# A rebuilt opening of a graph attention kernel: rows of h prepared two parts ahead, and the second quad of h turned by the DMA queue

## The chip, the cores and the metric

The kernel runs on one core of one Trainium2 chip. The metric is the device time of one execution in microseconds (us). The times and the trace are those of the kernel before the change.

## The reference, cut to what matters

```python
h = relu(layernorm(x))                     # x: 4096 x 512, f32
q = h @ W_q.T + b_q;  k = h @ W_k.T + b_k;  v = h @ W_v.T + b_v
z = (q @ k.T) / sqrt(512)                  # 4096 x 4096
s = z * adj                                # adj: 4096 x 4096 of 0 and 1, f32, sparse
s = where(s == 0, -10000, s)
out = x + relu(softmax(s, axis=1) @ v)
```

The kernel never forms q and k. With M = W_k.T W_q the scores are h M h.T plus a term of the keys, (h . w), in which w comes from b_q and W_k; another vector u comes from b_k and W_q. M is a product of two f32 matrices (16 matmuls of 128x128 by 128x512). The other large products take f16 pairs (a high and a low half, three matmuls in the place of one).

## The kernel before, in words

**Tiles.** The 4096 rows are 32 tiles of 128, in 8 quads of 4 tiles, and in 16 pairs of 2. A block is 512 query rows. For the block's 512 columns, each pair of key tiles gives scores by seven products instead of eight (the functions `scores` and `product`, a Strassen-like scheme of 42 matmuls with 256 columns). After the opening, a main loop of 128 steps does for each step the scores of one pair (19 pairs ahead) and four products with v (`weigh_v`).

**Opening.** It makes M, w and u, normalises x into h, turns h so that its 512 features lie on the partitions, and makes for each tile `v` (`project_v`, 12 matmuls, 2.6 us) and for each quad and chunk of 128 features `g = M h` (`project_g`, 12 matmuls, 2.6 us). It is written out as "parts" k = 0, 1, 2, ...; part k = 4 g + i has the tile k for v, the chunk i of the quad g - 1 for g, and from part 9 on half of a pair's scores. Each engine has its own list of what it does in part k, in an order written by hand; nothing else schedules.

**One tile's way.** VectorE takes the statistics of a quad of x (`row_stats`, `aggregate`, `quad_var`), ScalarE the root (`square_root`), VectorE refines it (`quad_rstd`). ScalarE writes the normalised rows (`normalise`), then their high half (`high_h`), VectorE their low half (`low_h`) and the product with w (`row_dot`). Tiles 0 to 7 are turned by TensorE as f32 into PSUM (`transpose_h`) ahead of the split. The tiles from 8 on are split as rows into one of four row buffers and turned by a transposing DMA of SyncE's queue (`turn_h`). In part k the engines prepare tile k + 4.

**g.** ScalarE copies a chunk out of PSUM (`copy_g`), VectorE forms the four sums (`combine_g`, after chunks 1 and 3), ScalarE the high and VectorE the low half (`high_g`, `low_g`). In part 4 g this is done for the second half of the quad g - 2, and the scores of part 4 g + 1 wait for it. `store_g` writes the two pairs to DRAM.

**SyncE** issues every DMA from one list in order. An instruction that waits holds all that stand behind it. x is double buffered by quads; `load_x(q)` waits until the last tile of quad q - 2 is normalised.

**Scale.** Both v's weights and M are scaled by a power of two before the split. For that VectorE finds the largest absolute value, and GpSimd the largest over the partitions. w and u come from TensorE: four f32 matmuls each with 512 columns.

Of the kernel before, what the change touches and what calls it, by code (L numbers as in the profile page):

```python
# [5 lines left out]
F32 = mybir.dt.float32  # L6
# [5 lines left out]
ABSMAX = bass.bass_isa.ReduceOp.absmax  # L12
# [17 lines left out]
TURNED = 2 * QUAD  # L30
ROW_BUFS = 4
# [14 lines left out]
TINY = 1e-30  # L46
EXPONENT = 0x7F800000
WARM_UPS = 9
HEADROOM = (16.0, 4.0)
# [5 lines left out]
def adj_preln_attention(nc, x, adj_t, wq, bq, wk, bk, wv_t, bv, out, g_dram, v_dram, h_dram):  # L55
# [15 lines left out]
    with ctx:  # L71
# [16 lines left out]
        o_rows = sb("o_rows", [P, QUAD, DIM], F32)  # L88
        run_min = sb("run_min", [P, 2, QW], F32)
# [9 lines left out]
        zeros = sb("zeros", [P, P], F32)  # L99
        log_p = sb("log_p", [P, 1], F32)  # L100
# [7 lines left out]
        mag = [sb("mag_v", [P, KC], F32), sb("mag_m", [P, KC + 1], F32)]  # L108
        mag_all = [sb("mag_all_v", [P, KC], F32), sb("mag_all_m", [P, KC + 1], F32)]
# [24 lines left out]
        wv_pair = in_slots(16, 2).bitcast(F16).rearrange("p (s k n) -> p s k n", s=2, k=KC)  # L134
        m_pair = in_slots(18, 2).bitcast(F16).rearrange("p (s k n) -> p s k n", s=2, k=KC)
# [11 lines left out]
        h_rows = in_slots(10, 2).bitcast(F16).rearrange("p (u s n) -> p u s n", u=ROW_BUFS, s=2)  # L147
        p_hi = [p_buf[:, u, :, :] for u in range(3)]
        p_lo = [p_buf[:, 3 + u, :, :] for u in range(2)]
        x_quad = [o_rows[:, :, :],  # L150
# [4 lines left out]
        u_row = run_min[0:1, 0, :]  # L155
        bq_wide = row_acc[:, :].rearrange("p (k n) -> p k n", k=KC)
# [8 lines left out]
        u_row_bank = d_bank[0:1, :]  # L165
# [26 lines left out]
        wide_ready = sem("wide_ready")  # L192
# [5 lines left out]
        u_row_ready = sem("u_row_ready")  # L198
        u_row_copied = sem("u_row_copied")
# [4 lines left out]
        mag_ready = sem("mag_ready")  # L204
        mag_reduced = sem("mag_reduced")
# [136 lines left out]
        def gT_bank(q, i):  # L342
            return o_bank[1] if i % 2 == 1 else o_bank[3]
# [19 lines left out]
        def _(sp):  # L363
# [56 lines left out]
            def turn_h(t):  # L420
# [6 lines left out]
                sp.dma_start(quad_h(q)[:, :, :, span], h_rows[:, t % ROW_BUFS, :, :].rearrange("p s n -> p (s n)"),  # L427
# [10 lines left out]
            def store_out(s, a):  # L438
# [16 lines left out]
            load_first_x(1)
            load_wk(2)
            load_wk(3)
            load_first_x(2)
            load_first_x(3)
            for e in range(KC):  # L460
                sp.dma_start(wq_raw[:, e, :], wq[e * P:(e + 1) * P, :]).then_inc(wq_loaded[e], 16)
            sp.dma_start(wv_raw, wv_t.rearrange("(k p) n -> p k n", p=P)).then_inc(wv_loaded, 16)
            load_x(1)
# [5 lines left out]
            for g in range(QUADS + 1):  # L469
                if 1 <= g < QUADS:  # L470
                    store_h(g)
# [4 lines left out]
                if g >= 2:  # L476
                    store_g(2 * (g - 2))
                    store_g(2 * (g - 2) + 1)
                if 2 <= 2 * g - 3 < PAIRS:
                    load_adj(2 * g - 3)  # L480
                if 1 <= g < QUADS - 1:
                    turn_h(QUAD * g + QUAD)
                    turn_h(QUAD * g + QUAD + 1)
                if g < QUADS:
                    store_v(2 * g)
                if 1 <= g < QUADS - 1:
                    turn_h(QUAD * g + QUAD + 2)
                if g + 3 < QUADS:
                    load_x(g + 3)
                if 1 <= g < QUADS - 1:  # L490
                    turn_h(QUAD * g + QUAD + 3)
                if 2 <= 2 * g - 2 < PAIRS:
                    load_adj(2 * g - 2)
            store_g(PAIRS - 2)
# [39 lines left out]
        def _(pool):  # L534
            nc.gpsimd.memset(zeros[:, :], 0.0).then_inc(zeros_ready, 1)
            nc.gpsimd.memset(ident[:, :], 0.0).then_inc(ident_zero, 1)
# [19 lines left out]
            for k in range(2):  # L556
                pool.wait_ge(mag_ready, k + 1)
                nc.gpsimd.partition_all_reduce(mag_all[k][:, :], mag[k][:, :], P, ABSMAX).then_inc(mag_reduced, 1)
# [7 lines left out]
        def _(pe):  # L566
            def transpose_h(t):
                pe.wait_ge(normed, t + 1)
                if t >= 2:
                    pe.wait_ge(h_lo_ready, t - 1)  # L570
                if 2 <= t < QUAD + 2:
# [5 lines left out]
            def project_v(t):  # L577
# [4 lines left out]
                pe.wait_ge(wv_lo_ready, KC)  # L582
# [12 lines left out]
                for k in range(KC):  # L595
                    for m, (a, b) in enumerate(HI_LO):
# [4 lines left out]
            def project_g(q, i):  # L601
# [8 lines left out]
                elif q == 0 and i == 1:  # L610
                    pe.wait_ge(h_lo_ready, TURNED)
                else:
# [82 lines left out]
            def product_m(d):  # L695
                for e in range(KC):
                    if d == 0:
                        pe.wait_ge(wq_loaded[e], 16)
                    mm = pe.matmul(m_bank[d][:, :], wk_raw[:, e, d * P:(d + 1) * P], wq_raw[:, e, :],  # L699
                                   start=(e == 0), stop=(e == KC - 1))  # L700
                mm.then_inc(m_ready, 1)
# [4 lines left out]
            pe.wait_ge(wide_ready, KC)  # L706
# [948 lines left out]
```

## Time and profile before

| | |
|---|---|
| median of 3 runs | 1463.7 us (1463.51 to 1463.74) |
| profiled execution, its own time | 1463.89 us |
| its span in the trace | 1462.1 us |
| TensorE busy | 1449.8 us (99%) |
| VectorE busy | 1301.7 us (89%) |
| ScalarE busy | 868.2 us (59%) |
| granted TensorE clock | nine tenths or more of full speed in all 40 slices |

Busy time is the union of an engine's instructions. What a row calls idle is the time just before an instruction on the same engine. The first 300 us hold the opening; the main loop takes the rest.

### The profile page before, as it was taken

To read this page: it belongs to the slowest core of one execution; us is meant where nothing else is said; L and a number is where in the kernel's file an instruction comes from. 1 tells how busy PE (TensorE), PEld (TensorE's weight loads), DVE (VectorE), ACT (ScalarE), POOL (GpSimd) and SP (SyncE) were. 2 spreads that over 40 slices of the span, in tenths; PEclk is the share of its full clock that TensorE was granted. 3 is DMA by queue.
4 is the path that set the end of the run, shared out by engine and by line. 5 is a ranking of instruction groups with operands and counts; after the bars stand their busy time and mean duration, and the time that the engine had idled before them with its cause. 6 is when DMAs were issued, how large, how long until landed. Compare 5 with 4: busy or idle time off the path is not lost.

```text
span 1462.1 us, 24721 instructions
## 1 busy us (share of the span) xinstructions
PE 1449.8 (99%) x9414; PEld 924.2 (63%) x9414; DVE 1301.7 (89%) x1597; ACT 868.2 (59%) x1398; POOL 44.8 (3%) x27
## 2 busy tenths in 40 slices
PE   8999999999999999999999999999999999999999
PEld 4455556766666666666666666666666666666555
DVE  7979888898999899998989898989898999987986
ACT  4666666765656566655665565656566566655542
POOL 0000000000000000100010001000000001000100
PEclk9999999999999999999999999999999999999999
DMA  6587666375555665566556664666456655664252
GB/s 209 162 270 215 219 182 244 137 297 187 223 216 226 215 241 216 220 218 243 204 202 248 224 233 186 225 245 239 188 225 245 234 187 203 245 216 178 90 162 97
DMA packets 100533, 307.53 MB, mean 210 GB/s; under 512 B 33856, under 2 KB 34112, under 8 KB 98624
## 3 DMA queue, kind: packets, MB, share of 16 engines
q1 hardware_dynamic: 100416, 305.96, 58.5%
q8 instruction: 75, 1.23, 0.3%
q14 instruction: 42, 0.34, 0.1%
HBM read 260.84 MB, written 38.80 MB: 205 GB/s over the span
## 4 chain that ended last, share of the span: by engine, by line
PE 93%; DVE 4%; ACT 1%; issue 1%; DMA 0%; SPq 0%; POOL 0%; DVEq 0%; ACTq 0%
PE o L688 45%; PE za L630 22%; PE zd L630 11%; PE zb L630 5%; PE o L617 4%; PE o L597 4%; PE zb L688 1%; DVE stats L1117 1%; PE za L699 0%; DVE g_buf L1197 0%; DMA slots<-in_L_gnn_W_q 0%; ACT g_buf L839 0%; DVE slots L1291 0%; DVE slots L1169 0%; DVE slots L1287 0%
## 5 line engine op out<-in xcount | busy, mean ns | idle before, releaser
L688 PE MATMUL o<-v_buf,p_buf 128*128 128x512 f16 x3072 | 726.4, 376 | 0.8 <-DVE p_buf L1323 0.6
L688 PEld LDWEIGHTS o<-v_buf,p_buf 128*128 128x128 f16 x3072 | 300.5, 98 | 260.9 <-issue 1.5
L630 PE MATMUL za<-h_buf,g_buf 128*128 128x256 f16 x2952 | 402.2, 273 | 1.6 <-ACT um_tmp L888 0.7
L630 PEld LDWEIGHTS za<-h_buf,g_buf 128*128 128x128 f16 x2952 | 287.3, 98 | 140.0 <-DVE g_buf L1197 3.7
L630 PE MATMUL zd<-h_buf,g_buf 128*128 128x256 f16 x1476 | 201.3, 273 | 0.0
L908 ACT ACTIVATE slots<-slots,log_p 128x1024 f32<-128x1024 f32 x128 | 146.0, 1141 | 51.5 <-DVE slots L1316 51.4
L1323 DVE TENSOR_TENSOR p_buf<-slots,p_buf 128x1024 f16<-128x1024 f32 x128 | 157.4, 1230 | 14.5 <-PE zb L688 13.6
L1316 DVE TENSOR_TENSOR slots<-slots,floor_b 128x1024 f32<-128x1024 f32 x128 | 170.0, 1330 | 0.3 <-POOL floor_b L547 0.3
L1279 DVE TENSOR_TENSOR slots<-um_tmp,dm_tmp 128x512 f32<-128x512 f32 x128 | 89.2, 697 | 78.7 <-ACT dm_tmp L893 78.7
L903 ACT ACTIVATE slots<-za,c_all,kappa 128x256 f32<-128x256 f32 x128 | 72.2, 564 | 142.4 <-PE za L630 141.5
L1291 DVE SCALAR_TENSOR_TENSOR slots<-slots 128x1024 f32<-128x1024 f32 x128 | 156.0, 1219 | 0.2
L630 PEld LDWEIGHTS zd<-h_buf,g_buf 128*128 128x128 f16 x1476 | 144.4, 98 | 16.7
L866 ACT ACTIVATE mm_tmp<-za,c_all,kappa 128x256 f32<-128x256 f32 x128 | 72.5, 567 | 137.3 <-PE za L630 134.1
L915 ACT CAST p_buf<-slots 128x1024 f16<-128x1024 f32 x128 | 133.0, 1039 | 9.1 <-PE zb L688 8.6
L1337 DVE TENSOR_TENSOR acc<-acc,slots 128x1024 f32<-128x1024 f32 x112 | 137.1, 1224 | 0.3
L1303 DVE TENSOR_TENSOR run_min<-run_min,slots 128x1024 f32<-128x1024 f32 x112 | 136.4, 1218 | 0.2
L1287 DVE TENSOR_TENSOR slots<-slots,adj_own 128x1024 f32<-128x1024 f32 x92 | 115.8, 1259 | 12.7 <-ACT slots L903 5.1
L878 ACT ACTIVATE um_tmp<-za,c_all,kappa 128x256 f32<-128x256 f32 x128 | 72.5, 566 | 55.4 <-PE za L630 50.8
L888 ACT ACTIVATE um_tmp<-za,c_all,kappa 128x256 f32<-128x256 f32 x128 | 72.4, 566 | 54.1 <-PE za L630 53.7
L630 PE MATMUL zb<-h_buf,g_buf 128*128 128x256 f16 x738 | 100.7, 273 | 0.0
L630 PEld LDWEIGHTS zb<-h_buf,g_buf 128*128 128x128 f16 x738 | 72.2, 98 | 8.3
L597 PE MATMUL o<-slots,h_buf 128*128 128x512 f16 x288 | 66.1, 379 | 1.3 <-DVE v_buf L1177 1.3
(155 smaller groups left out, 1121.8 us busy)
## 6 DMA issues: line engine op xcount, KB each, us to landing
g_buf<-g_dram SPq DMA_DIRECT2D x108, 896.0 KB, 5.5
v_buf<-v_dram SPq DMA_DIRECT2D x128, 512.0 KB, 3.4
adj_own<-in_adj SPq DMA_DIRECT2D x92, 512.0 KB, 6.2
spare<-in_adj SPq DMA_DIRECT2D x36, 512.0 KB, 6.3
g_dram<-g_buf SPq DMA_DIRECT2D x12, 896.0 KB, 5.5
v_dram<-v_buf SPq DMA_DIRECT2D x16, 512.0 KB, 4.7
spare<-in_x SPq DMA_DIRECT2D x15, 512.0 KB, 7.5
h_buf<-h_dram SPq DMA_DIRECT2D x7, 1024.0 KB, 8.8
```

Source lines behind the costliest of these rows:

```text
L597: mm = pe.matmul(v_bank(t)[:, :], h[:, a, k, span], wv_pair[:, b, k, :], start=(k == 0 and m == 0), stop=(k == KC - 1 and m == 2))
L630: mm = pe.matmul(bank[:, 0:QH], g_of(i)[:, a, op, j, :], right[b][j], start=(fresh and j == 0 and m == 0), stop=(j == 1 and m == 2), skip_ ...
L688: mm = pe.matmul(bank, a[:, kt, span], v_buf[:, n % V_BUFS, kt, b, c:d], start=(j == 0 and kt == 0 and m == 0), stop=(j == PAIRS - 1 and k ...
L908: nc.scalar.activation(slot(n), slot(n), ACT.Exp, bias=log_p[:, 0:1], scale=-UNIT).then_inc(p_ready, 1)
L915: nc.scalar.copy(p_hi[n % 3], slot(n)).then_inc(p_hi_ready, 1)
L1279: v.tensor_tensor(slot(i)[:, 1, :], um_tmp[:, :, :].rearrange("p a n -> p (a n)"), dm_tmp[:, :, :].rearrange("p a n -> p (a n)"), ALU.add) ...
L1287: v.tensor_tensor(slot(i), slot(i), adj_buf[adj_slot(i)], ALU.mult).then_inc(weighted, 1)
L1291: v.scalar_tensor_tensor(out=slot(i), in0=slot(i), scalar=0.0, in1=slot(i), op0=ALU.is_equal, op1=ALU.subtract).then_inc(negated, 1)
L1303: v.tensor_tensor(run_min[:, :, :], run_min[:, :, :], slot(i), ALU.min).then_inc(min_seen, 1)
L1316: v.tensor_tensor(slot(n), slot(n), floor_b[:, :].unsqueeze(1).to_broadcast([P, 2, QW]), ALU.add).then_inc(lowered, 1)
L1323: v.tensor_tensor(p_lo[n % 2], slot(n), p_hi[n % 3], ALU.subtract).then_inc(p_lo_ready, 1)
L1337: v.tensor_tensor(acc[:, :, :], acc[:, :, :], slot(n), ALU.add).then_inc(summed, 1)
```

## The change

Five edits to the opening. The main loop is not touched.

1. **Loads.** `b_q` and `b_k` come laid out as 128 x 4, and the halves of W_k and W_q come in turns. W_v comes ahead of the last quarter of W_k and W_q.
2. **M, w and u.** The 16 f32 products run quarter by quarter as the weights land. w and u are summed by ScalarE and VectorE over the four quarters (`add_w`, `add_u`), and TensorE sums over the partitions with a matrix of ones: one matmul for w and four with one column for u.
3. **Scale.** The largest absolute value gives way to a root of the sum of squares: five ScalarE instructions with squares, one matmul with one column, one all-reduce of GpSimd.
4. **h of the second quad** goes the way of the later ones: `TURNED` is 4 now, so TensorE transposes tiles 0 to 3 only, and tiles 4 to 31 are turned by the DMA queue, from two row buffers.
5. **Two parts ahead.** In part k the engines prepare tile k + 2. The statistics of a quad move from the parts with i = 1 to those with i = 3, `quad_rstd` from i = 3 to i = 1, `key_terms` from i = 3 to i = 1, the root from i = 2 to i = 0.

```diff
-TURNED = 2 * QUAD
-ROW_BUFS = 4
+TURNED = QUAD
+ROW_BUFS = 2
...
+        def row_tile(k):
+
+            return k + 2 if k + 2 < TILES else -1
...
+            products_m(0, 0, 3)
+            products_m(1, 0, 3)
+            products_m(2, 0, 3)
+            pe.wait_ge(ones_ready, 1)
+            pe.wait_ge(square_v_ready, 1)
+            pe.matmul(norm_bank, ones[:, :], square[0][:, 0:1], start=True, stop=True).then_inc(square_v_summed, 1)
+            pe.wait_ge(w_part_ready, KC)
+            pe.matmul(w_bank[:, :], ones[:, :], w_part, start=True, stop=True).then_inc(w_ready, 1)
+            products_m(3, 0, 0)
             pe.wait_ge(ident_ready, 1)
             transpose_h(0)
+            products_m(3, 1, 2)
             transpose_h(1)
...
+            products_m(3, 3, 3)
+            pe.wait_ge(u_part_ready, KC)
             for d in range(KC):
-                mm = pe.transpose(u_bank[:, d:d + 1], u_row[:, d * P:(d + 1) * P], ident[0:1, 0:1])
+                mm = pe.matmul(u_bank[:, d:d + 1], u_part[:, d * P:(d + 1) * P], ones[:, 0:1], start=True, stop=True)
             mm.then_inc(u_ready, 1)
...
+            for t in range(QUAD):
+                project_v(t)
+                if t + 2 < TURNED:
+                    transpose_h(t + 2)
...
             def magnitude(k):
-                dve.wait_ge(mag_reduced, k + 1)
-                link(v.tensor_reduce(top[k][:, :], mag_all[k][:, :], AX_X, ALU.max))
+
+                dve.wait_ge(norm_ready, k + 1)
...
-                if i == 3 and 1 <= g and g + 2 < QUADS:
-                    quad_rstd(g + 2)
...
+                if i == 1 and g + 1 < QUADS:
+                    quad_rstd(g + 1)
...
-                if g + 1 < QUADS:
-                    low_h(k + QUAD)
+                if row_tile(k) >= 0:
+                    low_h(row_tile(k))
...
-                if g >= 2 and i == 1 and g + 2 < QUADS:
+                if i == 3 and g + 2 < QUADS:
                     for t in range(QUAD):
                         row_stats(QUAD * (g + 2) + t)
```

**VectorE, parts 15 and 16** (L1287/L1333 weighs a pair by adj, L1153/L1202 is `row_dot`, L1291/L1337 negates, L1182 to L1190 or L1231 to L1239 `combine_g`). Before:

```order
L1287 TENSOR_TENSOR slots<-slots,adj_own 128x1024
L1153 SCALAR_TENSOR_TENSOR half_min,dots<-acc,floor_b 128x512
L1291 SCALAR_TENSOR_TENSOR slots<-slots 128x1024
L1160 TENSOR_SCALAR c_all<-dots,bq_bk 128x4
L1182 TENSOR_TENSOR slots<-slots 128x256
```

and now:

```order
L1333 TENSOR_TENSOR slots<-slots,adj_own 128x1024
L1202 SCALAR_TENSOR_TENSOR half_min,dots<-acc,floor_b 128x512
L1337 SCALAR_TENSOR_TENSOR slots<-slots 128x1024
L1166 BN_STATS stats<-p_buf 128x6 x4
L1172 BN_AGGR mean_var<-stats 128x2 x4
L1177 COPY mean<-mean_var 128x4
L1178 TENSOR_SCALAR var_eps<-mean_var 128x4
L1231 TENSOR_TENSOR slots<-slots 128x256
```

The ten instructions of the statistics now stand between the negation of part 15 and the sums of g in part 16. Before they stood two parts earlier.

**SyncE, from the load of the third quad of x on.** Before:

```order
L370 DMA o_rows<-in_x 128x4x512
L380 DMA adj_own<-in_adj 128x1024 x2
L414 DMA v_dram<-v_buf 128x2048
L370 DMA p_buf<-in_x 128x4x512
L436 DMA h_dram<-h_buf 128x4096
L414 DMA v_dram<-v_buf 128x2048
L427 DMA_TRANSPOSE h_buf<-slots 128x8x128 x2
```

and now:

```order
L384 DMA o_rows<-in_x 128x4x512
L394 DMA adj_own<-in_adj 128x1024 x2
L428 DMA v_dram<-v_buf 128x2048
L441 DMA_TRANSPOSE h_buf<-p_buf 128x8x128
L441 DMA_TRANSPOSE h_buf<-h_row_own 128x8x128
```

The first transposes, those of tiles 4 and 5, stand right behind the load of x, two loads of adj and a store of v.

**SyncE, group g = 3** (L418/L432 is `store_g`). Before:

```order
L418 DMA g_dram<-g_buf 128x3584
L418 DMA g_dram<-spare 128x3584
L380 DMA adj_own<-in_adj 128x1024
L427 DMA_TRANSPOSE h_buf<-slots 128x8x128 x2
L414 DMA v_dram<-v_buf 128x2048
```

and now:

```order
L432 DMA g_dram<-g_buf 128x3584
L432 DMA g_dram<-spare 128x3584
L441 DMA_TRANSPOSE slots<-p_buf 128x8x128
L384 DMA p_buf<-in_x 128x4x512
L394 DMA adj_own<-in_adj 128x1024
L441 DMA_TRANSPOSE slots<-h_row_own 128x8x128
```

The transpose behind the stores was that of tile 16, used in part 16. Now it is that of tile 14, used in part 14.

## Rows read from the trace of the kernel before

**Rows 1.** The page: the chain that ended last, by engine.
```profile
PE 93%; DVE 4%; ACT 1%; issue 1%; DMA 0%; SPq 0%; POOL 0%; DVEq 0%; ACTq 0%
```

**Rows 2.** Stretches: length, each engine's busy time, clock, DMA share, GB/s.
```profile
31.50:47.00 15.50, 14.84 (x77) 7.63 (x75) 14.57 (x38) 8.73 (x16) 0.39 (x1) 1.00 0.26 101
47.00:60.70 13.70, 13.27 (x61) 5.77 (x62) 13.27 (x37) 7.83 (x13) 0.00 (x0) 1.00 0.66 194
60.70:73.00 12.30, 10.68 (x48) 4.52 (x48) 11.47 (x26) 8.98 (x16) 0.00 (x0) 1.00 0.55 129
104.00:134.50 30.50, 30.35 (x184) 17.52 (x182) 26.10 (x55) 20.50 (x36) 0.00 (x0) 1.00 0.74 232
```

**Rows 3.** The timeline of TensorE, opening: start, duration, instruction.
```profile
16.19 3.59 PE L717 MATMUL zd<-slots,b_cols 128*1 128x512 f32 x8
19.71 1.09 PE L574 MATMUL o<-ident,acc 128*128 128x128 f32 x8
24.51 3.70 PE L699 MATMUL zb<-slots 128*128 128x512 f32 x8
31.48 2.75 PE L597 MATMUL o<-slots,h_buf 128*128 128x512 f16 x12
73.11 0.83 PE L630 MATMUL za<-h_buf,g_buf 128*128 128x256 f16 x6 [0.68 <-DVE g_buf L1197]
```

**Rows 4.** DMA of the first 20 us: GB/s in 0.5 us, one issue.
```profile
GB/s 0 0 0 1 28 127 373 209 315 254 207 42 87 242 348 402 393 393 406 397 406 410 410 402 381 389 389 385 381 389 385 389 393 385 393 381 356 148 25 33
slots<-in_L_gnn_W_v SPq DMA_DIRECT2D x1, 1024.0 KB, 8.4
```

**Rows 5.** The scales of v's weights (timeline), and a wide ScalarE group (page).
```profile
23.77 2.56 ACT L926 ACTIVATE slots<-slots,up 128x512 f16<-128x512 f32 x4
26.58 2.73 DVE L1390 SCALAR_TENSOR_TENSOR slots<-slots,up 128x512 f16<-128x512 f32 x4
...
L908 ACT ACTIVATE slots<-slots,log_p 128x1024 f32<-128x1024 f32 x128 | 146.0, 1141 | 51.5 <-DVE slots L1316 51.4
```

**Rows 6.** The timeline of parts 13 to 17: VectorE, ScalarE, TensorE.
```profile
113.12 2.47 DVE L1117 BATCH_NORM_STATS2 stats<-p_buf 128x6 f32<-128x512 f32 x4
116.05 0.42 DVE L1182 TENSOR_TENSOR slots<-slots 128x256 f32<-128x256 f32 x1
129.16 0.42 DVE L1182 TENSOR_TENSOR slots<-slots 128x256 f32<-128x256 f32 x1
131.47 1.76 ACT L839 CAST g_buf<-slots 128x896 f16<-128x896 f32 x2
133.57 0.83 PE L630 MATMUL za<-h_buf,g_buf 128*128 128x256 f16 x6
```

**Rows 7.** TensorE: the scores of part 13, and v of tile 14.
```profile
103.19 0.83 PE L630 MATMUL za<-h_buf,g_buf 128*128 128x256 f16 x6
112.31 2.75 PE L597 MATMUL o<-slots 128*128 128x512 f16 x12
```

**Rows 8.** Stores of g (page); one store, the transpose behind it, one alone.
```profile
g_dram<-g_buf SPq DMA_DIRECT2D x12, 896.0 KB, 5.5
...
L418 SPq DMA_DIRECT2D g_dram<-g_buf x1: 1240/1240/1240, 74.4 to 74.4; - x1
DMA to landing us min/median/max: 7.7/7.7/7.7
...
L427 SPq DMA_TRANSPOSE slots<-slots x1: 2765/2765/2765, 75.7 to 75.7; - x1
DMA to landing us min/median/max: 9.1/9.1/9.1
...
L427 SPq DMA_TRANSPOSE h_buf<-slots x1: 1244/1244/1244, 151.7 to 151.7; - x1
DMA to landing us min/median/max: 3.1/3.1/3.1
```

**Rows 9.** VectorE's idle time in part 28.
```profile
229.16 0.69 DVE L1177 TENSOR_TENSOR v_buf<-o,v_buf 128x512 f16<-128x512 f32 x1 [1.71 <-ACT v_buf L816]
```

More of the change, by code:

```diff
@@ L99, in adj_preln_attention @@
         zeros = sb("zeros", [P, P], F32)
+        ones = sb("ones", [P, P], F32)
         log_p = sb("log_p", [P, 1], F32)
@@ L693, in weigh_v, with products_m @@
                 mm.then_inc(o_done, 1)
[L695 to L698, printed above, removed]
+            def products_m(e, first, last):
+                pe.wait_ge(wk_loaded[e], 16)
+                pe.wait_ge(wq_loaded[e], 16)
+                for d in range(first, last + 1):
                     mm = pe.matmul(m_bank[d][:, :], wk_raw[:, e, d * P:(d + 1) * P], wq_raw[:, e, :],
                                    start=(e == 0), stop=(e == KC - 1))
-                mm.then_inc(m_ready, 1)
+                    if e == KC - 1:
+                        mm.then_inc(m_ready, 1)
             pe.wait_ge(zeros_ready, 1)
@@ L899, in copy_c12 @@
                     act.wait_ge(summed, added(i - SLOTS))
-                if i in (10, 11):
-                    for t in range(TILES - ROW_BUFS, TILES):
-                        act.wait_ge(h_turned[t % ROW_BUFS], turned(t))
                 nc.scalar.activation(slot(i)[:, 0, QH:QW], a_bank[i % 2][:, 0:QH], ACT.Identity, bias=key_term(i, 0),
@@ L941, in _ @@
+            nc.scalar.activation(top[0][:, :], norm_bank, ACT.Sqrt).then_inc(norm_ready, 1)
+            normalise(1)
+            high_wv(0)
+            high_h(0)
+            high_wv(1)
             act.wait_ge(w_ready, 1)
             nc.scalar.copy(w_all, w_bank[:, :]).then_inc(w_copied, 1)
-            normalise(0)
-            normalise(1)
-            high_h(0)
+            high_wv(2)
+            high_wv(3)
             high_h(1)
             normalise(2)
+            square_m(0)
+            square_m(1)
@@ L958, in _ @@
-            for k in range(KC):
-                high_wv(k)
-            square_root(1)
-            normalise(4)
-            for k in range(PARTS):
+            normalise(4)
+            square_m(3)
+            act.wait_ge(u_copied, 1)
+            nc.scalar.activation(u_square[:, :], u_cols[:, :], ACT.Square, scale=U_SHARE,
+                                 accum_out=square[1][:, KC:KC + 1]).then_inc(square_m_ready, 1)
+            high_h(4)
+            high_v(2)
+            keep_h(3)
+            act.wait_ge(square_sum_ready, 1)
@@ L964, in _ @@
+            nc.scalar.activation(top[1][:, :], square_sum[:, :], ACT.Sqrt).then_inc(norm_ready, 1)
+            normalise(5)
+            high_m(0)
+            high_m(1)
+            high_m(2)
+            high_m(3)
+            high_h(5)
+            high_v(3)
+            normalise(6)
+            for k in range(QUAD, PARTS):
                 g, i = k // QUAD, k % QUAD
@@ L1265, in add_c11 @@
                 dve.wait_ge(m2_copied, i + 1)
-                if i in (10, 11):
-                    for t in range(TILES - ROW_BUFS, TILES):
-                        dve.wait_ge(h_turned[t % ROW_BUFS], turned(t))
                 if i >= SLOTS:
@@ L1490, in _ @@
                     low_g(g - 1, i - 2)
-                if k == 2:
-                    low_m(0)
-                    low_m(1)
+                if k == QUAD:
+                    for t in range(2 * QUAD, 3 * QUAD):
+                        row_stats(t)
+                    for t in range(2 * QUAD, 3 * QUAD):
+                        aggregate(t)
+                    quad_var(2)
                 if k == 4:
```

288 lines of the change are left out of this document (150 added, 138 removed).

## Prediction, written before the result was known

> **What bounds the kernel now.** I read the page's chain first. TensorE holds 93% of it [rows 1], so time is saved only where TensorE waits or where work leaves its queue, and an edit to the opening counts by how much earlier, or later, TensorE gets through to the main loop. Next come the stretches. From v of tile 0 at 31.48 to the first scores at 73.11 [rows 3] there are 41.5 us. TensorE is busy for 38.8 of them and VectorE for 39.3 (14.57 + 13.27 + 11.47 [rows 2]), and the last wait in it, 0.68 us ahead of the first scores, is for VectorE's `low_g` [rows 3]. The opening has two bounds there that lie on top of each other. In parts 13 to 16 TensorE is full (30.35 of 30.5) and VectorE has 4.4 us of room in four parts [rows 2]. All sums are made against the profiled execution, 1463.9 us with a span of 1462.1; the median is 0.2 lower.
>
> **What is removed from TensorE.** w costs four f32 matmuls, u four more; the eight rows of u's are 3.59 us [rows 3], 0.9 for one. w keeps one, so 2.7 go; u keeps four of one column, some 1.2 by my estimate (eight loads of f32 weights, of which TensorE spaces 0.14 to 0.19), so 2.4 go. Four transposed tiles at 0.55 (1.09 for two [rows 3]) are 2.2. Together 7.3 us. If TensorE's own work were the bound, this would be the gain, and more with the waits.
>
> **When v of tile 0 starts now.** Between 7 and 18 us the queues move about 390 GB/s; W_v, issued at 8.0, landed 8.4 us later [rows 4], at 16.4, behind 4.2 MB. Now 3.7 MB are ahead of its end, and the two slow loads of b with 4-byte pieces (the dip to 42 and 87 GB/s [rows 4]) are gone. I take 13.8. ScalarE then squares 2048 columns, 2.2 us (1141 ns for 1024 [rows 5]): 16.0. A normalisation (0.8), the root and VectorE's four links (0.2 and 0.8) give the scale at 17.9. ScalarE's four high halves at 0.64 and VectorE's four low halves at 0.68 [rows 5], with h of tile 0, w and one `row_dot` between them, end at 23.2. TensorE would be free at 22.6 (5.2 for the first landing, 14 us of products, 3 us of the rest). u's columns are copied by VectorE behind the last low half, and v of tile 0 waits for that copy: 23.5. That is 8.0 earlier than 31.48, give or take 1.5.
>
> **From there to the first scores.** VectorE's work in this stretch hardly changes. Gone are three reductions of M (1.8). New are two more statistics and one more quad's end (1.2 and 0.5), one `low_h` and one `row_dot` (0.6 and 0.7): +1.3 net. So 23.5 + 41.5 + 1.3 = 66.3, if VectorE waits no more than before. Two waits are new.
>
> The first is the queue. The load of the third quad of x now waits for the normalisation of tile 3, at about 30, and with it two loads of adj; 2.6 MB with the store of v stand ahead of the transpose of tile 4 (the second order shown). They need 6.7 us at 390 GB/s, so v of tile 4 starts at about 40, and TensorE, done with tile 3 at 36, stands still for 4. VectorE meanwhile has M's low halves to do and loses 2.4. The Trainium skill says of this (DMA: Bandwidth & Descriptors, section Queues, rings and completion order) that each DMA engine consumes descriptors in ring order. The trace agrees: a transpose alone landed in 3.1 us, one issued right behind two stores of g in 9.1, 2.7 us after the second store [rows 8]. By the other rule of the skill, that transposing DMAs are as fast as plain ones (Advanced Engine Details and Errata, section X-Bar Transpose (TRN2)), only the bytes ahead would matter, and the 2.7 would be about 1.
>
> The second is ScalarE, which carries five squares more, some 3 us. I take 1.0 (bounds 0 and 2.6). First scores: 66.3 + 2.4 + 1.0 = 69.7 against 73.1. **Term 1: -3.4**, bounds -8.9 (VectorE never waits, v at 23) and +1.8 (the transpose 1.9 later, v 1.5 later, ScalarE 1.6 more).
>
> **The statistics moved to i = 3.** The block takes 2.93 us (113.12 to 116.05 [rows 6]). In its old place it costs little: ScalarE waits for the sums of g that follow. In its new place (the first order shown) it stands ahead of the sums on which the next scores depend. Before, the sums start at 129.16, ScalarE's halves at 131.47 and the scores at 133.57 [rows 6]. Between `low_h` of that part and the sums stand 3.6 us of work, so `low_h` started at 125.5. Now VectorE, without the block behind it, comes to it 1 us earlier, at 124.5, where ScalarE's half holds it. From there: 0.6, 1.1, 0.7, 1.1, the block 2.93, the sums 1.55, together 8.0. ScalarE can start at 132.6, which is 1.1 later, and so is TensorE. For the first quad (part 11) VectorE had waited before, nothing is caught up, and it is 1.4. The moved `quad_rstd` (0.9) falls into idle time at i = 1. This comes four times, in parts 11, 15, 19 and 23: 1.4 + 3 x 1.1. The block in part 7 is in term 1. **Term 2: +4.7**, bounds 0 (all of it hidden by room elsewhere) and 5.6 (1.4 each).
>
> **Two parts ahead, two row buffers.** The tile 4 g + 2 is now turned right behind two stores of g (the third order shown) and used in part 4 g + 2. From the scores that open part 13 to v of tile 14 there are 9.1 us (103.19 to 112.31 [rows 7]). The stores are issued 1.0 and 1.4 us after the start of these scores. The second takes 5.5 (the median) to 7.7 to land, and the transpose lands up to 2.7 after it [rows 8]; for the lower end I take 0.8, an estimate, 3.1 for one alone less the part that runs beside the store. That is 7.7 to 11.8, around the 9.1: in five groups a wait of 0 to 2.7 each. I take 0.1 each, near the median store, since here the queue is empty ahead of the stores, as it was not at 74.4: **term 3: +0.5**, bounds 0 and 13.5. High halves that wait for a row buffer wait for a transpose whose v is already through, at no cost.
>
> **The end of the opening.** `low_h` and `row_dot` of tiles 30 and 31 fall into parts 28 and 29, 1.3 us each on VectorE. Part 28 has 1.71 idle [rows 9] and hides the first; after part 29 VectorE is full for 20 us. **Term 4: +0.8**, bounds 0 and 1.4.
>
> **Sum.** 1463.9 - 3.4 + 4.7 + 0.5 + 0.8 = 1466.5; less 0.2 for the median, 1466.3. In the main loop TensorE is the bound throughout, so a shift at 300 us is a shift at the end.
>
> **Rivals.**
>
> A, faster. TensorE's queue is the bound from v of tile 0 on: the transpose of tile 4 isn't held (the loads of x and adj are through, or share the engines with it), VectorE fills every gap, and the block of statistics is hidden. For it: TensorE and VectorE differ by half a microsecond in the stretch. Against it: the last wait is VectorE's. It gives -7.3 for the work gone, +1 for the block: 1457.4. It decides if the first scores start before 67 and terms 2 and 3 together stay under 2.
>
> B, no change. Term 1 holds without the wait for tile 4 (-5.8), terms 2 to 4 as worked out (+6.0): 1463.9. For it: VectorE is busy anyway while TensorE waits. Against it: rows 8.
>
> C, slower by more. The transpose behind the stores lands 10.8 us after the scores' start, 1.7 late, in each of five groups: 5 x 1.7 = 8.5 in place of 0.5, so 1474.3. For it: rows 8. Against it: that transpose also had stores of h and v ahead.
>
> **How the numbers follow.** A measurement here tells about 0.2% (2.9 us) from no change. Forecast 0.45, A 0.22, B 0.20, C 0.13. The forecast's own range is 1462 to 1471, and its middle lies at the bound itself: 0.26 slower, 0.18 the same, 0.01 faster. A is 0.20 faster, 0.02 the same. B is 0.02 slower and 0.18 the same, with a little taken from it for a better term 2 (0.02 faster, in the place of the slower part). C is slower. Faster 0.23, the same 0.37, slower 0.40. The range runs from 1457.5 to 1472: it takes in all but the outer half of A and most of C.
>
> **What would show it.** v of tile 0 at 22 to 25; v of tile 4 at 38.5 to 41, waiting for a transpose; the first scores at 67 to 72, waiting for `low_g`; waits of 1.1 to 1.4 for `low_g` ahead of the scores of parts 13, 17, 21 and 25; small waits or none ahead of v of tiles 10, 14, 18, 22, 26. I am wrong if the scores' waits stay under 0.3 (then term 2 is hidden), or if v of tile 4 starts by 38 (then the queue isn't FIFO here).

## The result and the profile after

| | before | after |
|---|---|---|
| median of the runs, us | 1463.80 (1463.51 to 1464.06, 6 runs) | 1473.03 (1471.86 to 1476.46, 6 runs) |
| profiled execution, us | 1463.9 | 1472.2 |
| its span, us | 1462.1 | 1470.4 |
| TensorE busy, us | 1449.8 | 1443.5 |

The changed kernel is slower: ratio 1.0066, 95% interval 1.0055 to 1.0077, 9.2 us by the medians and 8.3 by the profiled executions. The forecast was 1466.3 with a range to 1472.0, so the direction was that of the forecast's own middle, and the size lies 1.0 above the range.

TensorE is busy for 6.3 us less and ends 8.3 later, so it stands idle for 14.6 us more, and the page names the waits. First its chain (compare [rows 1]), then two groups of its costliest ones, whose last field is the idle time ahead of the group and what ended most of it:

```profile
PE 89%; DVE 5%; DMA 2%; ACT 2%; issue 1%; SPq 0%; POOL 0%; DVEq 0%; ACTq 0%
...
L652 PE MATMUL za<-h_buf,g_buf 128*128 128x256 f16 x2952 | 402.4, 273 | 8.9 <-DVE g_buf L1246 8.1
...
L618 PE MATMUL o<-slots,h_buf 128*128 128x512 f16 x288 | 67.5, 386 | 7.8 <-DMA h_buf<-p_buf 6.7
```

The scores (L652) waited 8.1 us for `low_g` on VectorE (L1246), and v (L618) waited 6.7 us for transposed tiles. The timeline of TensorE shows where; these are its waits of over 0.4 us from 20 us to the main loop, but for one of g (1.27 at 52.49) and one of 0.69 at 303.06 that the kernel before has too (0.68). Brackets hold the idle time before the row and what ended it:

```profile
24.05 2.75 PE L618 MATMUL o<-slots,h_buf 128*128 128x512 f16 x12 [0.98 <-issue]
41.77 4.27 PE L618 MATMUL o<-slots,h_buf 128*128 128x512 f16 x12 [5.75 <-DMA h_buf<-p_buf]
73.42 0.83 PE L652 MATMUL za<-h_buf,g_buf 128*128 128x256 f16 x6 [2.34 <-DVE g_buf L1246]
104.92 0.83 PE L652 MATMUL za<-h_buf,g_buf 128*128 128x256 f16 x6 [1.44 <-DVE g_buf L1246]
136.51 0.83 PE L652 MATMUL za<-h_buf,g_buf 128*128 128x256 f16 x6 [1.44 <-DVE g_buf L1246]
168.27 0.83 PE L652 MATMUL za<-h_buf,g_buf 128*128 128x256 f16 x6 [1.44 <-DVE g_buf L1246]
178.54 2.76 PE L618 MATMUL o<-slots,h_buf 128*128 128x512 f16 x12 [0.98 <-DMA h_buf<-p_buf]
200.93 0.83 PE L652 MATMUL za<-h_buf,g_buf 128*128 128x256 f16 x6 [1.44 <-DVE g_buf L1246]
249.82 0.83 PE L652 MATMUL za<-h_buf,spare 128*128 128x256 f16 x6 [1.07 <-ACT um_tmp L899]
254.33 0.83 PE L652 MATMUL za<-h_buf,spare 128*128 128x256 f16 x6 [0.44 <-ACT um_tmp L909]
```

Reading the starts against those of before gives the account. v of tile 0 is 7.4 us earlier than the 31.48 of [rows 3]. The first scores are 0.31 later than the 73.11 there: the whole gain is gone between the two. From then on the lateness grows at the places of the forecast. The scores of part 13 are 1.73 later than the 103.19 of [rows 7], those of part 17 2.94 later than the 133.57 of [rows 6]. The same rows of before for parts 21 and 25 start at 163.96 and 194.35, so they are 4.31 and 6.58 later. The main loop's first product of v starts at 305.82 against 297.48: 8.34 later, which is the 8.3 at the end.

The wait for tile 4 in detail. The transpose was issued at 34.19, behind a load of x of 1 MB, two of adj and a store of v, and landed at 41.7. This is its row in the timeline of SyncE's queue, and the DMA view of 28 to 44 us (the last figure is the median from issue to landing):

```profile
34.19 1.72 SPq L441 DMA_TRANSPOSE h_buf<-p_buf  x1
...
o_rows<-in_x SPq DMA_DIRECT2D x1, 1024.0 KB, 5.5
adj_own<-in_adj SPq DMA_DIRECT2D x2, 512.0 KB, 7.9
v_dram<-v_buf SPq DMA_DIRECT2D x2, 512.0 KB, 6.0
h_buf<-p_buf SPq DMA_TRANSPOSE x1, 7.5
h_buf<-h_row_own SPq DMA_TRANSPOSE x1, 3.2
```

And this is what the wait did to TensorE, by stretches (length, each engine's busy time, then the granted clock, DMA share and GB/s), and to VectorE (its timeline):

```profile
37.00:38.00 1.00, 0.00 (x0) 0.00 (x0) 1.00 (x3) 1.00 (x3) 0.00 (x0) 1.00 0.97 356
38.00:39.00 1.00, 0.00 (x0) 0.00 (x0) 1.00 (x2) 1.00 (x3) 0.00 (x0) 0.52 1.01 407
39.00:41.00 2.00, 0.00 (x0) 0.00 (x0) 1.97 (x5) 0.62 (x1) 0.00 (x0) 0.50 1.26 180
41.00:44.00 3.00, 2.23 (x6) 0.85 (x7) 0.00 (x0) 0.00 (x0) 0.00 (x0) 0.50 0.90 264
44.00:45.00 1.00, 1.00 (x4) 0.33 (x3) 0.00 (x0) 0.00 (x0) 0.00 (x0) 0.57 0.00 0
45.00:46.00 1.00, 1.00 (x6) 0.49 (x5) 0.00 (x0) 0.00 (x0) 0.00 (x0) 1.00 0.00 0
...
46.70 0.69 DVE L1226 TENSOR_TENSOR v_buf<-o,v_buf 128x512 f16<-128x512 f32 x1 [5.73 <-ACT v_buf L837]
```

TensorE is idle from 36.0; right behind 38 its granted clock is down to half (1.2 of 2.4 GHz), and it is full again only shortly before 45, so that the twelve matmuls of v take 4.27 us and not 2.75. VectorE's list stands at the low half of this v, and VectorE is idle for 5.73.

The block of statistics in its new place is seen ahead of the scores of part 17 (timelines of VectorE and ScalarE, to be laid beside [rows 6]; TensorE's row is the one of 136.51 above):

```profile
126.39 0.69 DVE L1218 TENSOR_TENSOR h_row_own<-acc,h_row_own 128x512 f16<-128x512 f32 x1 [1.02 <-ACT h_row_own L826]
129.89 2.46 DVE L1166 BATCH_NORM_STATS2 stats<-p_buf 128x6 f32<-128x512 f32 x4
132.81 0.42 DVE L1231 TENSOR_TENSOR slots<-slots 128x256 f32<-128x256 f32 x1
134.40 1.78 ACT L860 CAST g_buf<-slots 128x896 f16<-128x896 f32 x2 [1.31 <-DVE slots L1239]
135.37 2.10 DVE L1246 TENSOR_TENSOR g_buf<-slots,g_buf 128x896 f16<-128x896 f32 x2 [0.40 <-ACT g_buf L860]
```

ScalarE waits for the sums (L1231 to L1239), which waited for the block, and TensorE for both. The sums start 3.65 later than the 129.16 of [rows 6], for scores that come 2.94 later.

### The profile page after: what moved, and what is told of

Same layout as the page of the kernel before. It is cut to its first block, busy times and chain, and to the rows that moved or that the text cites. A ratio compares the mean times of both kernels' runs of the same rounds, so it can differ in the third digit from the quotient of the medians.

```text
span 1470.4 us, 24697 instructions
## 1 busy us (share of the span) xinstructions
PE 1443.5 (98%) x9390; PEld 921.6 (63%) x9390; DVE 1299.7 (88%) x1588; ACT 873.2 (59%) x1413; POOL 44.6 (3%) x27
## 4 chain that ended last, share of the span: by engine, by line
PE 89%; DVE 5%; DMA 2%; ACT 2%; issue 1%; SPq 0%; POOL 0%; DVEq 0%; ACTq 0%
PE o L710 44%; PE za L652 21%; PE zd L652 11%; PE zb L652 5%; PE o L618 4%; PE o L639 2%; DMA h_buf<-p_buf 2%; DVE stats L1166 1%; PE zb L710 1%; DVE g_buf L1246 1%; DMA slots<-in_L_gnn_W_v 1%; DVE slots L1333 0%; DVE slots L1337 0%; ACT g_buf L860 0%; ACT h_row_own L826 0%
## 5 line engine op out<-in xcount | busy, mean ns | idle before, releaser
L652 PE MATMUL za<-h_buf,g_buf 128*128 128x256 f16 x2952 | 402.4, 273 | 8.9 <-DVE g_buf L1246 8.1
L652 PEld LDWEIGHTS za<-h_buf,g_buf 128*128 128x128 f16 x2952 | 287.3, 98 | 147.1 <-DVE g_buf L1246 11.1
L652 PE MATMUL zd<-h_buf,g_buf 128*128 128x256 f16 x1476 | 201.4, 273 | 0.0
L1337 DVE SCALAR_TENSOR_TENSOR slots<-slots 128x1024 f32<-128x1024 f32 x128 | 156.0, 1219 | 0.1
L652 PEld LDWEIGHTS zd<-h_buf,g_buf 128*128 128x128 f16 x1476 | 144.4, 98 | 16.8
L1333 DVE TENSOR_TENSOR slots<-slots,adj_own 128x1024 f32<-128x1024 f32 x92 | 115.8, 1259 | 12.6 <-ACT slots L921 5.0
L652 PE MATMUL zb<-h_buf,g_buf 128*128 128x256 f16 x738 | 100.7, 273 | 0.0
L652 PEld LDWEIGHTS zb<-h_buf,g_buf 128*128 128x128 f16 x738 | 72.2, 98 | 8.4
L618 PE MATMUL o<-slots,h_buf 128*128 128x512 f16 x288 | 67.5, 386 | 7.8 <-DMA h_buf<-p_buf 6.7
```

The costliest lines, as they stand in the source:

```text
L618: mm = pe.matmul(v_bank(t)[:, :], h[:, a, k, span], wv_pair[:, b, k, :], start=(k == 0 and m == 0), stop=(k == KC - 1 and m == 2))
L652: mm = pe.matmul(bank[:, 0:QH], g_of(i)[:, a, op, j, :], right[b][j], start=(fresh and j == 0 and m == 0), stop=(j == 1 and m == 2), skip_ ...
L1333: v.tensor_tensor(slot(i), slot(i), adj_buf[adj_slot(i)], ALU.mult).then_inc(weighted, 1)
L1337: v.scalar_tensor_tensor(out=slot(i), in0=slot(i), scalar=0.0, in1=slot(i), op0=ALU.is_equal, op1=ALU.subtract).then_inc(negated, 1)
```

## The experiments

Each was timed beside the kernel before, which gave 1463.6 to 1463.8 each time. "After" is the changed kernel, 1473.03, profiled execution 1472.2.

**e2_queue_late: SyncE's order in the opening.**

```
-            load_x(2)
-            load_adj(0)
-            load_adj(1)
             for g in range(QUADS + 1):
...
                     turn_h(QUAD * g + QUAD)
+                if g == 0:
+                    load_x(2)
...
                     turn_h(QUAD * g + QUAD + 1)
+                if g == 0:
+                    load_adj(0)
+                    load_adj(1)
```

> The changed kernel with three loads moved in SyncE's list: the load of the third quad of x behind the transpose of tile 4, the first two loads of adj behind the transpose of tile 5. Theory Q (the 2.6 MB ahead of it delay the transpose of tile 4 by some 4 us, and with it VectorE): it lands about 3.5 after its issue, v of tile 4 starts at 37.5 to 38.5 with under 2 us of waiting, TensorE's clock stays up, the first scores come at 68.5 to 70.5, and the time falls by 3 to 5, to about 1469. Rival (VectorE's own work decides the first scores whatever v of tile 4 does): v of tile 4 early, first scores at 72 to 73.5, time 1472 to 1473.

1467.01 (1465.71 to 1468.71, 11 runs), ratio to before 1.0022 [1.0013, 1.0031]; 6.0 below after. TensorE's timeline:

```profile
37.14 2.76 PE L620 MATMUL o<-slots,h_buf 128*128 128x512 f16 x12 [1.41 <-DMA h_buf<-p_buf]
68.38 0.83 PE L654 MATMUL za<-h_buf,g_buf 128*128 128x256 f16 x6 [1.63 <-DVE g_buf L1248]
```

The transpose of tile 4, issued at 33.91, lands in 3.2 us with no load ahead of it (the store of v, issued at 31.07, is through), against 7.5 in after. The wait is 1.41, the clock stays full and v takes 2.76. The first scores are 5.04 earlier. So the three loads ahead of one transpose cost 5.0 us at the first scores and 5.2 at the end. By the medians it is 6.0; in the profiled execution of after v of tile 4 took 4.27, and the same v took 5.30 in those of e1, e3 and e4, so that the profiled execution may be one of the milder ones.

**e8_turned8: no transposes of the queue in the second quad.** TensorE turns tiles 4 to 7 as in the kernel before; the rest is as in after.

```
-TURNED = QUAD
+TURNED = 2 * QUAD
```

(beside it, the transposes of the four tiles are issued after the scores two parts earlier, and SyncE leaves them out)

> The changed kernel with its headline edit alone undone: TensorE transposes tiles 4 to 7 too (as f32 into PSUM, ahead of the split), and the DMA queue turns tiles from 8 on. Theory Q: no wait for a transpose ahead of v of tile 4, TensorE's clock stays up, 2.0 us of transposes more on TensorE's queue where VectorE is the bound; first scores at 69 to 71, about 1469.5. Rival (TensorE's four transposes cost what they save, VectorE decides): 1472 to 1474.

1466.59 (1466.02 to 1469.11, 10 runs), ratio 1.0023 [1.0013, 1.0032]. First scores at 68.55, the four waits of 1.44 as in after. Two quite different ways to be rid of the wait for tile 4 bring the first scores to within 0.2 us of each other. The 2.2 us of TensorE's work that e8 puts back cost nothing that can be seen at the first scores. My 1469.5 was too high, because it priced the wait for tile 4 as low as the forecast had.

**e6_fill_wait and e6b_fill24: the clock alone.** Zero matmuls fill TensorE's wait for tile 4 (44 of them, then 24):

```
+                if k == QUAD:
+                    pe.wait_ge(h_kept, 3)
+                    for _ in range(24):
+                        pe.matmul(o_bank[0][:, 0:P], zeros[:, :], zeros[:, :], start=True, stop=True)
```

> The changed kernel with 44 small matmuls of zeros ahead of v of tile 4, into a bank that is free, so that TensorE works for most of the time in which it waits for the transpose. Theory C (the granted clock fell to half because TensorE stood idle, and v of tile 4 took 4.3 instead of 2.7 us): the clock stays at 1.0, v of tile 4 takes 2.75, all that follows is 1.5 earlier, about 1471.5. Rival (the 1.5 us are hidden by other waits ahead of the first scores): the first scores stay at 73.4, 1473. If the small matmuls take longer than the wait, v of tile 4 starts later, and this is seen in the trace.

> 24 f32 matmuls of zeros (128x128) go into TensorE's queue ahead of v of tile 4, about 0.226 us each, 5.4 us in all, so that they fill the wait for the transpose but don't outlast it. Theory (the twelve matmuls of v took 4.27 us instead of 2.75 because the granted clock fell to 0.5 in the wait): v of tile 4 starts at 41.8 as before, takes 2.75, first scores at 71.9, time 1470.7. Rival (the clock's fall is covered, VectorE is behind anyway): 1472.2.

With 44 the filler took 9.99 us and outlasted the wait: 1475.13 (1473.56 to 1476.73, 5 runs), ratio 1.0078 [1.0065, 1.0091]. v of tile 4 ended 2.4 us later than in after (48.5) and the first scores started 2.4 later (75.84). With 24 it fitted: 1471.54 (1471.30 to 1472.44, 5 runs), ratio 1.0055 [1.0043, 1.0068]. The timeline of e6b_fill24:

```profile
35.90 5.52 PE L763 MATMUL o<-zeros 128*128 128x128 f32 x48
41.56 2.76 PE L618 MATMUL o<-slots,h_buf 128*128 128x512 f16 x12
...
71.70 0.83 PE L652 MATMUL za<-h_buf,g_buf 128*128 128x256 f16 x6 [2.34 <-DVE g_buf L1250]
```

v of tile 4 starts 0.2 earlier than in after, takes 2.76 at the full clock, and the first scores are 1.72 earlier, as is the end of v. So of the 5.0 us some 1.5 are the clock's, 3.5 the wait's; and in both experiments the first scores follow the end of v of tile 4 one for one. A filler recovers less than moving the loads, since the wait stays. The gain of 1.5 by the medians is not certain (the intervals of e6b and after overlap), and the profiled execution ends only 0.7 below that of after: behind the first scores v of tiles 10 and 18 waited 0.65 and 1.52 for their transposes, where in after v of tile 22 waited 0.98.

**e1_stats_i2 and e3_stats_i0: the place of the statistics.** e1 moves the block one part earlier (`i == 3` to `i == 2`). e3 puts it right behind the sums, a part later:

```
-                if i == 3 and g + 2 < QUADS:
+                if i == 0 and 2 <= g < QUADS - 1:
                     for t in range(QUAD):
-                        row_stats(QUAD * (g + 2) + t)
+                        row_stats(QUAD * (g + 1) + t)
```

(and so for `aggregate` and `quad_var`; ScalarE's `square_root(g + 1)` follows at `i == 1`)

> The changed kernel with one line altered: the statistics of a quad stand at the end of the parts with i = 2 and not i = 3. Theory S (the block ahead of the sums of g costs a wait for low_g of 1.44 us in each of parts 13, 17, 21, 25): the four waits fall to 0.2 or less, the first scores stay at 73 to 74, and the time falls by 4.5 to 5.5, to about 1468. Rival (VectorE has no room anywhere, so the block costs the same wherever it stands): the waits move to other instructions, and the time stays within 1 us of 1473.

> Only the place of the block of statistics: for quads 3 to 6 it runs at the end of the parts with i = 0, right behind the sums and low_g that the scores wait for, instead of at the end of parts with i = 3, right ahead of them; ScalarE's root follows in the next part. Theory S (VectorE stands behind the block when the scores need low_g, and has no time to catch up): the four waits of 1.44 us ahead of the scores of parts 13, 17, 21 and 25 (104.92, 136.51, 168.27, 200.93) fall to 0.3 or less each, the later starts of the main loop shrink by about 4 x 1.3, and the time is 1472.2 - 5.2 = 1467.0. Rival (the waits come from ScalarE or from VectorE's total work, not from the order): the waits return elsewhere in the same group of parts, ahead of v or g, and the time stays at 1471 to 1473.

e1: 1471.95 (1468.79 to 1472.47, 5 runs), ratio 1.0051 [1.0039, 1.0064], an interval that overlaps that of after. Three of the four waits fell from 1.44 to 0.72, one went; neither of the expectations. The block is still ahead of the same sums, and one part of room takes up half of it. Its profiled opening was worse than that of after (first scores at 74.60, v of tile 4 at the half clock for 5.30 us, v of tile 8 late by 1.02), which hides part of the gain, though the wait ahead of the first scores fell too, from 2.34 to 1.14. From the first scores to the main loop it took 229.7 us against 232.4.

e3: 1465.42 (1464.36 to 1468.14, 11 runs), ratio 1.0015 [1.0006, 1.0024], 7.6 below after. Timelines of VectorE and TensorE at part 17:

```profile
126.04 0.42 DVE L1231 TENSOR_TENSOR slots<-slots 128x256 f32<-128x256 f32 x1
130.10 2.09 DVE L1246 TENSOR_TENSOR g_buf<-slots,g_buf 128x896 f16<-128x896 f32 x2 [0.77 <-ACT g_buf L860]
134.80 2.46 DVE L1166 BATCH_NORM_STATS2 stats<-p_buf 128x6 f32<-128x512 f32 x4
...
131.25 0.83 PE L652 MATMUL za<-h_buf,g_buf 128*128 128x256 f16 x6
```

The same 2.9 us of work, behind `low_g`: the scores wait for nothing, and all five waits are gone, that of the first scores too (71.08), because the block of part 7 stood ahead of those. From the first scores to the main loop 226.9 us, 5.5 less than after. The expectation of 1467.0 had counted four blocks, and this was the fifth.

**e4_turn_first: the transpose ahead of the stores of g.**

```
+                if 1 <= g < QUADS:
+                    turn_h(QUAD * g + 2)
                 if g >= 2:
                     store_g(2 * (g - 2))
                     store_g(2 * (g - 2) + 1)
-                if 1 <= g < QUADS:
-                    turn_h(QUAD * g + 2)
```

> Only SyncE's order: the transpose of tile 4g + 2 is issued ahead of the two stores of g, not behind them. Theory (a transpose lands when the bytes ahead of it are through): it lands 3 to 4 us after its issue instead of 5.6 to 9.9, the wait of 0.98 ahead of v of tile 18 goes, and the time is about 1471 (1472.2 - 1.0). Rival: the 1 us is taken up by the wait for low_g that follows, and the time stays within 0.3 of 1472.2. If the stores of g, now later by 0.6 to 1.8 us, held anything up, it would be slower.

1471.52 (1469.88 to 1473.63, 5 runs), ratio 1.0055 [1.0042, 1.0067]. In after the transposes behind the stores took 5.6 to 9.9 us to land (the last row below is the one of 232.9); ahead of them, in e4, all six took 3.0 to 3.2 (the first row is that of 75.8):

```profile
DMA to landing us min/median/max: 3.0/3.0/3.0
...
DMA to landing us min/median/max: 9.9/9.9/9.9
```

The wait of 0.98 is gone; it stood ahead of v of tile 22, not 18 as written in the expectation. The profiled execution shows one way in which five runs of such a kernel come to spread over 4 us. TensorE waited 2.35 us ahead of the first scores, as in after, but here the granted clock fell right behind that wait:

```profile
74.00:80.00 6.00, 5.76 (x26) 3.11 (x27) 3.13 (x10) 2.84 (x6) 0.00 (x0) 0.72 0.55 175
```

v of tile 9 then took 3.64 us in place of 2.75. The gain of the move itself, 1.5 by the medians, is not certain: the intervals of e4 and after overlap. e14 below measures it again.

**e9_all_moves, e9_again, e14_no_turn: together.** e9 is e2, e3 and e4 in one; e14 is e9 without e4's move.

> Three moves of order together: the load of the third quad of x and two loads of adj behind the transposes of tiles 4 and 5 (measured alone: -5.2 to -6.0), the statistics at the end of parts with i = 0 (expected -5.2), the transpose of tile 4g + 2 ahead of the stores of g (-1.0). If the three are independent: 1472.2 - 6.0 - 5.2 - 1.0 = 1460.0, with the first scores at 68.4 and no wait over 0.5 ahead of later scores up to 200 us. If TensorE's earlier work only meets VectorE sooner, the waits ahead of the scores return at 0.5 to 1 each: 1463.

> The kernel of e9_all_moves again, beside e15_short_dots on the same chip: 1459.3, 4.3 below before.

> e9_all_moves without its third move: the transpose of tile 4g + 2 stays behind the two stores of g. Theory (term 3 costs about 1 us): waits of 0.3 to 1.5 for transposes ahead of one or two of v of tiles 10, 14, 18, 22, 26, and 1460.3. With the waits for low_g gone TensorE comes to these v 1.44 earlier, so that more of the five could wait: up to 1464. Rival: below 0.3, the same as 1459.3.

e9: 1459.31 (1458.69 to 1460.24, 7 runs) and again 1459.87 (1459.09 to 1460.60, 7 runs), ratio 0.9971 [0.9960, 0.9982] and 0.9972 [0.9962, 0.9983]. That is 4 us faster than the kernel before and some 13 faster than after. e14: 1460.30 (1459.43 to 1461.76, 11 runs), ratio 0.9977 [0.9968, 0.9986], with waits for transposes of 1.04 at 168.04 (tile 22 again) and of 0.4 to 0.7 at four other tiles that aren't turned right behind stores of g, beside that for tile 4; the third move is worth some 0.4 to 1.0 us by the medians, with intervals that overlap. TensorE's timeline in e9 (first profile):

```profile
23.97 2.75 PE L620 MATMUL o<-slots,h_buf 128*128 128x512 f16 x12 [0.98 <-issue]
37.35 2.76 PE L620 MATMUL o<-slots,h_buf 128*128 128x512 f16 x12 [1.42 <-DMA h_buf<-p_buf]
65.73 0.83 PE L654 MATMUL za<-h_buf,g_buf 128*128 128x256 f16 x6
236.86 0.83 PE L654 MATMUL za<-h_buf,spare 128*128 128x256 f16 x6 [1.07 <-ACT um_tmp L901]
241.37 0.83 PE L654 MATMUL za<-h_buf,spare 128*128 128x256 f16 x6 [0.44 <-ACT um_tmp L911]
```

The first scores are 7.4 us earlier than before, and nothing waits for `low_g` any more. The main loop starts at 292.86, 4.6 earlier than before. So 2.8 of the 7.4 are given back on the way: 1.5 in the two waits at 236.86 and 241.37, and 1.2 in two waits for transposes (0.72 and 0.49).

**e10_c2_first and e15_short_dots: the end of the opening.** e10 is e9 with the sum that frees `um_tmp` ahead of two operations of `combine_t` in part 31, and so in part 32. e15 is e9 with `row_dot` of tiles 30 and 31 over 16 columns, not 512, which leaves out most of the product with w for these two tiles.

```
 e10
-                if 29 <= k < 33:
+                if k in (29, 32):
                     combine_t(1, k - 29)
...
                     add_c2(whole)
+                if k in (31, 32):
+                    combine_t(1, k - 30)
 e15
+                n = DIM if t < TILES - 2 else 16
```

> e9_all_moves with one more change of order on VectorE: in part 31 the sum that frees um_tmp and dm_tmp (`add_c2`) stands ahead of the two operations of `combine_t(1, 1)`, not behind them. Theory (term 4: VectorE, which carries low_h and row_dot of tiles 30 and 31 now, comes late to that sum, ScalarE's copies of L901 and TensorE's scores wait for it): the wait of 1.07 at 236.86 goes, the one of 0.44 at 241.37 may grow by as much as VectorE still lacks, and the time is 1459.3 - 1.0 = 1458.3. Rival (VectorE is simply full from there to 290 us): the wait moves to the next scores and the time stays within 0.3 of 1459.3.

> e9_all_moves, with `row_dot` of tiles 30 and 31 cut to 16 of their 512 columns (part of the computation is left out: two tiles' key terms are wrong). It takes 0.6 us of VectorE's work out of part 28 and as much out of part 29. Theory (term 4: VectorE's late sum behind the work of tiles 30 and 31 makes the waits of 1.07 and 0.44 at 236.86 and 241.37): VectorE is up to 1.2 us earlier there, the two waits fall together to 0.3 to 0.5, and the time is 1459.3 - 1.1 = 1458.2. Rival (the waits come from the order around them, as combine_t and add_c2, whatever stands ahead): they stay at 1.5 together and the time at 1459.3. If only the row_dot of tile 31 counts, 0.6 less.

e10: 1459.60 (1458.71 to 1460.54, 7 runs), the same as e9. Its rival was right: the wait of 1.07 went, and that of 0.44 became 1.21. e15: 1459.45 (1458.46 to 1460.08, 6 runs), not to be told from e9_again beside it. Its profile:

```profile
237.66 0.83 PE L654 MATMUL za<-h_buf,spare 128*128 128x256 f16 x6 [0.58 <-ACT um_tmp L901]
242.17 0.83 PE L654 MATMUL za<-h_buf,spare 128*128 128x256 f16 x6 [0.43 <-ACT um_tmp L911]
```

The first wait fell by 0.49, the second not at all. Of the 1.0 us that this took from VectorE (each `row_dot` 0.5 shorter) only the half in part 29 counts. The half in part 28 became idle time, as the forecast had it: VectorE's wait ahead of the next `low_v` grew from 0.50 to 1.01. The second wait doesn't hang on these two `row_dot`. What makes it, I have not settled: `low_h` of tile 31 is the candidate that no run took away.

## Why the prediction was wrong

The sum of the profiled executions, term by term. A term's measured value is the growth of the lateness across its stretch.

| term | forecast | its bounds | measured in after |
|---|---|---|---|
| 1, to the first scores | -3.4 | -8.9 to +1.8 | +0.3 |
| 2, statistics at i = 3 | +4.7 | 0 to 5.6 | +5.3 (1.42 + 1.21 + 1.37 + 1.29) |
| 3, transposes behind stores | +0.5 | 0 to 13.5 | +1.0 |
| 4, end of the opening | +0.8 | 0 to 1.4 | +1.8 |
| sum | +2.6 | | +8.3 |

The places were those of the forecast. Terms 1 to 3 lie inside their own bounds and term 4 is 0.4 outside; the range, to 1472.0, was drawn far tighter than the bounds together. The failed step is in term 1, 3.7 of the 5.7 us that are missing: the wait for the transpose of tile 4, of which VectorE was to lose 2.4 us and lost 5.73.

VectorE's own account of the stretch from v of tile 0 to the first scores shows it (length, then TensorE, its weight loads, VectorE, ScalarE; before, then after):

```profile
31.48:73.11 41.63, 38.81 (x186) 17.95 (x184) 39.44 (x100) 25.65 (x44) 0.39 (x1) 1.00 0.48 142
...
24.05:73.42 49.37, 39.52 (x177) 17.33 (x177) 40.66 (x107) 29.84 (x57) 0.46 (x1) 0.93 0.57 160
```

The start is 7.4 us earlier (forecast 8.0), VectorE's work grows by 1.2 (forecast 1.3), and its idle time from 2.2 to 8.7, by 6.5 (forecast 2.4 for the queue and 1.0 for ScalarE). Of these 6.5, 5.7 are the one wait at tile 4.

- *v of tile 0 at 23.5.* It came at 24.05. Right within its 1.5.
- *"66.3, if VectorE waits no more than before."* The +1.3 of work was right, as the account above shows. The 66.3 itself was not reached by a run with the same work ahead of the first scores: e2, in which the queue alone is mended, has them at 68.38, with 40.4 us of VectorE's work in the stretch and 4.0 idle. e9's 65.73 is no test of it, since there the block of part 7 stands behind these scores.
- *"TensorE ... stands still for 4. VectorE meanwhile has M's low halves to do and loses 2.4."* This is the step that failed. The transpose landed 7.5 us after its issue and v of tile 4 started at 41.77, not at 40: the wait was 5.75. The low halves of M (36.4 to 39.2) lay beside it, but VectorE was through with all that it had by 41 and then idle for 5.73, so nearly the whole wait was VectorE's too. And v itself took 1.5 longer at the half clock, which the forecast had not in it at all. e2 prices the three together at 5.0 in place of 2.4, and in e2 TensorE still waits 1.41 for this transpose.
- *"The block in part 7 is in term 1."* Its work is in the +1.3 of that term, and the work came out. What its place costs was worked out for the four later parts and not for this one: e3 has it behind these scores, and the wait of 2.34 ahead of them is gone. That is a gain which the forecast didn't see, not a part of the miss, as the sum of VectorE's work had the block in the stretch already.
- *ScalarE's squares, +1.0.* Not shown either way. ScalarE is busy for 4.2 us more in the stretch (29.84 against 25.65), but no run takes the squares away. VectorE's idle time outside the wait at tile 4 grew by 0.8, and what made it stays open.
- *Term 2.* Right, and its mechanism too. Four waits of 1.44 made the lateness grow by 1.42, 1.21, 1.37 and 1.29, where 1.4 and three times 1.1 had been worked out. `low_h` of part 15 started 21.5 us behind the scores of part 13 (126.39 and 104.92) and, by the prediction's 125.5, 22.3 behind them before: 0.9 sooner, held by ScalarE's half (1.02), as forecast. From there to ScalarE's start at 134.40 are the 8.0 us of the forecast. e3 shows the cause of the waits, the order on VectorE.
- *Term 3.* From the start of the scores the five transposes landed after 8.8, 9.2, 9.3, 10.2 and 8.3 us (issued at 75.22, 108.52, 138.33, 170.09 and 202.7, landing 7.0, 5.6, 7.5, 8.4 and 6.5 later), inside the 7.7 to 11.8 that had been worked out, around the window of 9.1. One was late, by 0.98, and not all five by 0.1. Which one is late, and by how much, changes from one execution to the next: in the profiled executions that leave this order as it is, from nothing (e8) to 2.2 us in all (e6b). Rival C would have needed all five late by more.
- *Term 4.* One low half and one `row_dot` in part 29 were to cost 0.8 of 1.3; the waits are 1.51 together. e15 ties 0.5 to the one `row_dot`. The rest of it is open, as said, and so are the 0.3 by which the lateness grew beyond these two waits.

Three sums on the way are a little off and decide nothing: the stretch before is 41.63 us long, not 41.5; TensorE's 5.2 + 14 + 3 give 22.2, not 22.6; and the three items of term 1's upper bound give +1.6, not +1.8.

The rivals. A (TensorE's queue the bound, 1457.4) fell with v of tile 4 and with the waits for `low_g`; but the runs reach 1459.3 once the order on two queues is mended, so the work that the change takes from TensorE is real. B rested on VectorE being busy while TensorE waits; the 5.73 us of idle time deny it. C's time, 1474.3, is close to the measured one by luck: its mechanism isn't what happened.

Of the signs named in advance, v of tile 0, the waits of the four scores (1.44, at the top of 1.1 to 1.4), and what the scores wait for came out. v of tile 4 (38.5 to 41) was 0.8 outside, the first scores (67 to 72) 1.4 outside. The Trainium skill (DMA: Bandwidth & Descriptors, section Queues, rings and completion order) says that a DMA engine takes descriptors in the order of the ring. The runs agree: with the same loads behind it and not ahead, the same transpose landed in 3.2 us and not 7.5 (e2).

## What to carry to other kernels

When a change shortens one engine's work by moving work in the queues of others, look in each queue at what now stands ahead of the one instruction that the longest chain waits for, and do so at every repetition of the pattern, the first above all. Here 2.9 us of work cost nothing behind such an instruction, and ahead of it TensorE waited 1.4 to 2.3 each time. And a wait of several microseconds on TensorE isn't priced by its length alone: look at the granted clock of the stretch behind it.

## What the runs showed of the hardware

- *The clock.* TensorE, idle from 36.0 in after, still had its full clock in the stretch to 38, was at half of it right behind, and had it back about 3 us after it had begun to work again at 41.77; 1.5 us lost in one v. In e1, e3 and e4 the same twelve matmuls took 5.30. A wait of 1.41 at the same place (e2) left the clock alone; waits of 2.34 and 2.35 ahead of the first scores left it alone in after, and in e4 it was lowered right behind (0.72 over 74 to 80). The spread of after's six runs is 4.6 us against 0.55 of before. The mean granted clock, which is on record for every run, bears out that the clock is a part of it: it is 1.0 in all runs of before beside the experiments and in all of e9, and 0.995 to 0.998 in after, where the slowest run, 1476.46, has the 0.995. In e2 and e8 the three slowest runs of each are the three with 0.999, and the others have 1.0. It is not the whole, since e9 spreads over 1.5 us at 1.0.
- *Transposes on the queue.* 3.0 to 3.2 us from issue to landing with no transfer under way ahead of them (e2, e4), 5.6 to 9.9 right behind two stores of 0.9 MB each, 7.5 behind 2.6 MB (after).
- *Small f32 matmuls.* 24 of 128x128, recorded as 48, took 5.52 us: 0.23 each.
